# Four-layer MetaFormer: the first token group's work of the second and third expert layers moved into the stage before them

## The reference

```python
t = t + moe(layernorm(t))
scores = t @ gate_w + gate_b;  probs = softmax(scores)       # 4 experts
masked = probs * top2_mask;    masked /= masked.sum() + 1e-9
h = gelu(t @ w1[e] + b1[e]);   y[e] = h @ w2[e] + b2[e]      # 96 -> 384 -> 96
out = sum over e of masked[e] * y[e]
```

## Time and profile before

| | |
|---|---|
| median of 3 runs | 1336.79 us (1335.22 to 1337.23) |
| time of the profiled execution | 1334.63 us |
| its span | 1332.8 us |
| mean granted TensorE clock | 0.929 |
| second expert layer, first DVE instruction to the last addition to X | 523.4 to 703.4 us |
| third expert layer, the same | 904.4 to 1084.7 us |

### The profile page before, as it was taken

How to read it: one execution, slowest core, us unless ns; L and a number is a source line. 1 busy time by engine, 2 the same in 40 slices (tenths; PEclk the granted TensorE clock), 3 DMA queues, 4 the chain that set the end, 5 groups by cost and what they waited for, 6 DMA issues and landing times. The chain is left out here.

```text
span 1332.8 us, 23847 instructions
## 1 busy us (share of the span) xinstructions
PE 1177.9 (88%) x8368; PEld 1020.5 (77%) x8368; DVE 809.8 (61%) x2938; ACT 487.3 (37%) x948; POOL 249.9 (19%) x232
## 2 busy tenths in 40 slices
PE   2979999948999997999996999997999968998776
PEld 2978888937999996888894767676889867886455
DVE  6137676555666653767656665545767667776556
ACT  3524333314554543433331223224333322232542
POOL 3002212121010100221213343322121212111200
PEclk9989999967999998999996999997999988999577
DMA  3201010010000000000000000000000000000000
GB/s 136 76 24 49 14 47 0 0 48 1 1 2 1 2 1 1 1 1 0 0 1 0 1 1 2 1 1 1 1 1 0 0 1 1 1 1 1 3 10 36
DMA packets 11561, 15.67 MB, mean 12 GB/s; under 512 B 7385, under 2 KB 9007, under 8 KB 11346
## 3 DMA queue, kind: packets, MB, share of 16 engines
q1 hardware_dynamic: 10754, 12.86, 3.0%
q10 hardware_dynamic: 720, 1.66, 0.3%
HBM read 11.37 MB, written 3.15 MB: 11 GB/s over the span
## 5 line engine op out<-in xcount | busy, mean ns | idle before, releaser
L663 PEld LDWEIGHTS moe_dn<-all_w,moe_hid 128*128 128x128 f32 x2304 | 270.1, 192 | 5.9
L663 PE MATMUL moe_dn<-all_w,moe_hid 128*128 128x96 f32 x2304 | 271.5, 275 | 0.0
L600 ACT ACTIVATE moe_hid<-moe_up 128x512 f32<-128x512 f32 x288 | 169.7, 598 | 233.9 <-PE moe_up L655 221.8
L653 PE MATMUL moe_up<-moe_xh,moe_w1h 97*128 97x512 f32 x288 | 124.1, 431 | 0.0
L655 PE MATMUL moe_up<-moe_xl,moe_w1h 97*128 97x512 f32 x288 | 115.7, 402 | 0.0
L654 PE MATMUL moe_up<-moe_xh,moe_w1l 97*128 97x512 f32 x288 | 115.5, 401 | 0.0
L558 DVE SCALAR_TENSOR_TENSOR all_X<-moe_dn,moe_gate,all_X 128x96 f32 (+1 forms) x384 | 95.2, 310 | 33.4 <-PE moe_dn L663 29.1
L550 DVE SCALAR_TENSOR_TENSOR all_X<-all_b,moe_gate,all_X 128x96 f32 (+1 forms) x384 | 96.6, 314 | 10.8 <-DVE all_X L558 7.8
L481 POOL TENSOR_TENSOR moe_prob<-moe_euler,moe_logit 128x16 f32<-128x16 f32 x24 | 69.6, 2902 | 141.7 <-DVEq L517 141.7
L1060 PE MATMUL l1c_o<-l1c_vs,l1c_pt 128*128 128x64 f32 x768 | 94.4, 277 | 0.8 <-DVE l1c_ro L853 0.8
L1060 PEld LDWEIGHTS l1c_o<-l1c_vs,l1c_pt 128*128 128x128 f32 x768 | 91.8, 195 | 3.2 <-issue 1.4
(11 more groups left out here) (338 smaller groups left out, 2027.6 us busy)
## 6 DMA issues: line engine op xcount, KB each, us to landing
all_w<-w SPq DMA_DIRECT2D x3, 582.0 KB
all_w<-w SPq DMA_DIRECT2D x3, 576.0 KB
all_X<-x_rows SPq DMA_DIRECT2D x2, 768.0 KB, 6.7
conv_scratch<-all_X SPq DMA_DIRECT2D x2, 768.0 KB, 3.2
all_X<-conv_scratch SPq DMA_DIRECT2D x2, 768.0 KB, 4.7
out_tokens<-l3f_y SPq DMA_DIRECT2D x5, 288.0 KB, 2.1
l0c_band<-band ACTq DMA_DIRECT2D x1, 1248.0 KB, 9.2
all_b<-b SPq DMA_DIRECT2D x3, 192.0 KB
```

The lines of the kernel that those rows point to most:

```text
L600: act.activation(hid[:, n, :], up[n % UPS][:, :], ACT.Gelu).then_inc(hid_done, 1)
L653: pe.matmul(bank, w1h[:, n, :], xh[:, p, :], start=True, stop=False)
L663: last = pe.matmul(dn[e % 2][:, j * C:(j + 1) * C], hid[:, n, j * P:(j + 1) * P], w2[:, n, :], start=(k == 0), stop=(k == KC - 1))
```

## The change

The buffers and small tiles of an expert group are allocated once, ahead of the first expert layer, in a class `ExpertFront`. For layers 1 and 2 the start of the layer is gone: no statistics, normalisation, transposes, weight parts, low tokens or gates of group 0 there, and no memsets or rows of ones, which stay from layer 0. Each of these steps is called inside the program before, at a fixed stage:

- attention: ACT's weight copies at the end of stages 4 to 7, DVE's weight parts at the end of stages 7 to 10, statistics at the end of stage 4, POOL's power in its stage 5, normalisation at the end of stage 6; PE's transposes in stage 14, behind `scores(15, 1)`; ACT's copies, `dve_low` and `dve_gates` at the end of stage 14; PE's gate scores in stage 15, ahead of `values(15, 0)`; POOL's power for the gates behind its loop. The transposes and the scores use the PSUM bank m1, when it is out of use.
- second convolution: ACT's copies of the weights at the end of steps 2 to 5, DVE's parts at the end of steps 3 to 6, statistics at the end of step 3, POOL's power in step 4, normalisation at the end of step 4; transposes in step 7 behind `turn_values(6)`; ACT's copies behind `keys_out(7)`; gate scores behind `sample(6, 1)`; `dve_low` and `dve_gates` at the end of step 7; POOL's power behind its loop. The PSUM bank is tp.

`choose_experts` is the former `gates_of`, with the same operations in the same order. Layer 0 calls the same methods at its own start. The semaphores of group 0 are its own, so the counts of the others go down by one.

```diff
--- before.py
+++ after.py
+def choose_experts(dve, chain, F, scores, p, logit_done, gates_read, exp_done, count):
+    wide = lambda a: a.unsqueeze(2).broadcast_to([P, GT, NE])
+    smax, logit, prob, ge, rank, best = F.smax, F.logit, F.prob, F.ge, F.rank, F.gate[:, p, :, :]
+    chain.sync(dve.tensor_reduce(smax[:, :], scores, AX.X, ALU.max))
+    chain.sync(dve.tensor_tensor(logit[:, :, :], scores, wide(smax[:, :]), ALU.subtract))
+    dve.sem_inc(logit_done, 1)
+    dve.sem_inc(gates_read, 1)
+    for e in range(NE):
+        dve.memset(rank[:, :, e], float(NE - 1 - e))
+    wait(dve, exp_done, count)
...
+class ExpertFront:
...
+    def pool_rstd(self, pool):
+        pool.wait_ge(self.var_done, 1)
+        pool.tensor_tensor(self.rstd[:, :], self.var[:, :], self.mhalf[:, :], ALU.pow).then_inc(self.rstd_done, 1)
+    def pool_exp(self, pool):
+        pool.wait_ge(self.logit_done, 1)
+        pool.tensor_tensor(self.prob[:, :, :], self.euler[:, :].rearrange("p (t e) -> p t e", e=NE),
+                           self.logit[:, :, :], ALU.pow).then_inc(self.exp_done, 1)
+    def dve_stats(self, dve, chain):
+        layernorm_stats(dve, chain, [self.T["X"][:, j, :] for j in range(GT)], self.stats, self.mean, self.var, 1e-5)
+        dve.sem_inc(self.var_done, 1)
+    def dve_apply(self, dve, chain):
+        dve.wait_ge(self.rstd_done, 1)
+        layernorm_apply(dve, chain, [self.T["X"][:, j, :] for j in range(GT)], [self.xn[:, j, :] for j in range(GT)],
+                        self.stats, self.mean, self.rstd).then_inc(self.xn_done, 1)
+    def dve_weights(self, dve, e):
+        dve.wait_ge(self.w_high, e + 1)
+        dve.tensor_tensor(self.expert(self.w1l, e), self.expert(self.w1, e), self.expert(self.w1h, e).bitcast(F32),
+                          ALU.subtract).then_inc(self.w_low, 1)
+    def dve_low(self, dve):
+        dve.wait_ge(self.xt_done, 1)
+        dve.tensor_tensor(self.xl[0:C, 0, :], self.xt[0:C, 0, :], self.xh[0:C, 0, :].bitcast(F32), ALU.subtract
+                          ).then_inc(self.xl_done, 1)
+    def dve_gates(self, dve, chain):
+        dve.wait_ge(self.gates_in, 1)
+        choose_experts(dve, chain, self, self.gp.rearrange("p (t e) -> p t e", e=NE), 0, self.logit_done,
+                       self.gates_read, self.exp_done, 1)
+    def act_weights(self, act, e):
+        if e == 0:
+            act.wait_ge(self.loaded, 64)
+        act.activation(self.expert(self.w1h, e), self.expert(self.w1, e), ACT.Copy).then_inc(self.w_high, 1)
+    def act_tokens(self, act):
+        act.wait_ge(self.turned, 1)
+        act.activation(self.xh[0:C, 0, :], self.tp[0:C, :], ACT.Copy)
+        act.activation(self.xt[0:C, 0, :], self.tp[0:C, :], ACT.Copy).then_inc(self.xt_done, 1)
+    def pe_turn(self, pe):
+        pe.wait_ge(self.xn_done, 1)
+        for j in range(GT):
+            last = pe.transpose(self.tp[0:C, j * P:(j + 1) * P], self.xn[:, j, :], self.T["ident"][:, :])
+        last.then_inc(self.turned, 1)
+    def pe_gates(self, pe):
+        pe.wait_ge(self.loaded, 64)
+        pe.wait_ge(self.xt_done, 1)
+        for j in range(GT):
+            last = pe.matmul(self.gp[:, j * NE:(j + 1) * NE], self.xt[:, 0, j * P:(j + 1) * P], self.gw[:, :],
+                             start=True, stop=True)
+        last.then_inc(self.gates_in, 1)
...
@@ moe
-            with pool.Fori(0, STEPS) as g:
+            with pool.Fori(1, STEPS) as g:
                 rstd_of(g)
                 exp_of(g)
...
-            stats_of(0, chain)
-            apply_of(0, chain)
...
-            gates_of(0, 0, chain)
+            if layer == 0:
+                F.dve_stats(dve, chain)
+                F.dve_apply(dve, chain)
+                for e in range(NE):
+                    F.dve_weights(dve, e)
+                    if e == 0:
+                        F.dve_low(dve)
+                F.dve_gates(dve, chain)
+            dve.wait_ge(T["moe_in"][layer], 64)
             base = chain.n
             steps(dve, step)
...
-            act.wait_ge(T["moe_in"][layer], 64)
-            act.wait_ge(consts, 2)
-            act.activation(xh[C:CB, :, :], xt[C:CB, :, :], ACT.Copy)
-            act.activation(xl[C:CB, :, :], xt[C:CB, :, :], ACT.Copy, scale=0.0)
-            act.activation(expert(w1h, 0), expert(w1, 0), ACT.Copy).then_inc(w_high, 1)
-            turned_out(0, 0)
-            for e in range(1, NE):
-                act.activation(expert(w1h, e), expert(w1, e), ACT.Copy).then_inc(w_high, 1)
+            if layer == 0:
+                act.wait_ge(consts, 2)
+                act.activation(xh[C:CB, :, :], xt[C:CB, :, :], ACT.Copy)
+                act.activation(xl[C:CB, :, :], xt[C:CB, :, :], ACT.Copy, scale=0.0)
+                F.act_weights(act, 0)
+                F.act_tokens(act)
+                for e in range(1, NE):
+                    F.act_weights(act, e)
             gelus(0, 0)
...
             pe.wait_ge(T["moe_in"][layer], 64)
-            turn(0)
-            gates(0, 0)
-            pe.wait_ge(w_low, 1)
+            if layer == 0:
+                F.pe_turn(pe)
+                F.pe_gates(pe)
+                pe.wait_ge(F.w_low, 1)
+                pe.wait_ge(F.xl_done, 1)
             ups(0, 0, 0)
...
@@ -735,6 +815,7 @@
                  "unit_in", "unit_high", "unit_done", "v_in", "v_done", "scored", "maxed", "spread", "nm_in", "nm_high",
                  "nm_done", "st_in", "exped", "valued", "ro_done", "ht_in", "ht_done", "y_in", "added")
         S = {n: s.sem(n) for n in names}
+        F = T["front"].begin(s, T, 1, m1, m1[:, 0:GT * NE])
         block = ctx.enter_context(nc.Block())
         FIRST, SECOND = 8, NT // 2
 
@@ -782,6 +863,11 @@
                 if st == 0:
                     pool.wait_ge(S["x_low"], 4)
                     rstd_of(2, slice(SECOND, NT))
+                if st == 5:
+                    pool.wait_ge(S["x_low"], st + 4)
+                    F.pool_rstd(pool)
+            pool.wait_ge(S["x_low"], NB)
+            F.pool_exp(pool)
 
         @block.vector
         def _(dve):
@@ -908,6 +994,15 @@
                     maxima_low(st + 1)
                 if live(st - 1):
                     add_out(st - 1)
+                if st == 4:
+                    F.dve_stats(dve, chain)
+                if st == 6:
+                    F.dve_apply(dve, chain)
+                if 7 <= st < 7 + NE:
+                    F.dve_weights(dve, st - 7)
+                if st == NB - 2:
+                    F.dve_low(dve)
+                    F.dve_gates(dve, chain)
 
         @block.scalar
         def _(act):
@@ -974,6 +1069,10 @@
                     heads_out(st - 1)
                 if live(st + 1):
                     maxima_high(st + 1)
+                if 4 <= st < 4 + NE:
+                    F.act_weights(act, st - 4)
+                if st == NB - 2:
+                    F.act_tokens(act)
 
         @block.tensor
         def _(pe):
@@ -1106,6 +1205,11 @@
                 if live(st + 2):
                     unit(st + 2, 1)
                     value_tokens(st + 2)
+                if st == NB - 2:
+                    pe.wait_ge(S["unit_done"], 3 * NB)
+                    F.pe_turn(pe)
+                if st == NB - 1:
+                    F.pe_gates(pe)
                 if live(st):
                     values(st, 0)
                 if live(st + 3):
@@ -1194,6 +1298,7 @@
                  "pos_in", "th_done", "dist_done", "hat_done", "bil_done", "val_done", "vt_in", "vt_out", "k_in", "k_out",
                  "kb_done", "q_in", "q_out", "at_in", "at_out", "vb_in", "vb_out", "o_in", "o_out", "y_in", "y_out")
         S = {n: s.sem(n) for n in names}
+        F = T["front"].begin(s, T, 2, tp, tp[:, 0:GT * NE])
         block = ctx.enter_context(nc.Block())
 
         def live(p):
@@ -1251,10 +1356,13 @@
                 offsets_rstd(p)
                 if p in (0, 2):
                     rstd_of(2 + p // 2)
+                if p == 4:
+                    F.pool_rstd(pool)
                 for i in range(2):
                     keys(p, i)
                 for i in range(2):
                     bilinear(p, i)
+            F.pool_exp(pool)
 
         @block.vector
         def _(dve):
@@ -1362,6 +1470,15 @@
                 if p in (0, 2):
                     chain.sync(sums(*BATCHES[2 + p // 2]))
                     token_moments(2 + p // 2)
+                if p == 3:
+                    F.dve_stats(dve, chain)
+                if p == 4:
+                    F.dve_apply(dve, chain)
+                if 3 <= p < NP - 1:
+                    F.dve_weights(dve, p - 3)
+                if p == NP - 1:
+                    F.dve_low(dve)
+                    F.dve_gates(dve, chain)
 
         @block.scalar
         def _(act):
@@ -1450,6 +1569,8 @@
                     outputs_out(p - 1, 1)
                 if live(p + 1):
                     first_tap(p + 1)
+                if 2 <= p < 2 + NE:
+                    F.act_weights(act, p - 2)
 
```

(8 more changed lines are left out.)

167 lines of the change are left out of this document (81 added, 86 removed).

## The result

After the change the kernel takes **1340.58 us** (median of 9 runs, 1338.38 to 1344.36) against 1336.79 (also nine runs, 1335.22 to 1337.23); the ratio is 1.0032, with a 95% interval of 1.0022 to 1.0042. So it is slower by 3.8 us, 0.3%, inside the range and 2.1 us above the forecast. The profiled run took 1340.37 us with a span of 1338.6; against the profiled run of before (1334.63, span 1332.8) that is 5.8 us of span.

A forecast was written before the change was run, and what follows sets the result against it. Bound by TensorE in the stages and chains of small operations at the seams; first seam +1.8 and second -0.1 gave +1.7 us on the median 1336.79, so 1338.5 us, range 1332 to 1345.

The forecast's parts named there:

- Point 1: Gaps before the first up matmuls of layers 1 and 2: 8.55 to 0.6 us, gaining 8.0 us at each seam.
- Point 2: Attention's end: gates on VectorE delay norm_heads(14), so TensorE's values(15, 0) is held, +8.1 us.
- Point 3: Attention stage 14: four transposes on TensorE ahead of values(14, 0), +0.1 us (0 to 0.4).
- Point 4: Second convolution's end: gates wait for GpSimd's power behind bilinear, delaying add_output(6, 0) by 8.4 us, transposes and scores included.
- Point 5: Tails behind both holds: TensorE resumes at half clock, costing 3.0 us in the attention and 2.7 in the convolution.
- Point 6: Expert layers' starts: less time at half clock, gaining 0.9 us at the second layer and 2.6 at the third.
- point 7: First group of each layer: VectorE's bias sums start earlier, so the wait for group 1's tokens goes, gaining 0.7 us each.
- Point 8: Middle stages of attention and convolution: the moved preparation work is mostly covered by idle time, +0.3 us in all (0 to 2).
- the slower one: TensorE returns late from both holds, at half clock when the expert layer begins: 1345, or 1342 with half; chance 0.34.

The follow-up runs named there:

- its own run: Kernel before with only four transposes added in attention stage 14, ahead of values(14, 0): 1336.02 us, ratio 0.9993.
- moving the power: Changed kernel with GpSimd's power for the gates ahead of the last bilinear in the second convolution, not behind the loop: 1336.84 us, ratio 1.0003.
- the run with the attention's seam alone: Change made only between attention and second expert layer; third expert layer starts as in the kernel before: 1344.15 us, ratio 1.0051 against the kernel before.
- the seams run alone: Change made at one seam only, against the kernel before: attention's 1344.15 us, ratio 1.0051; second convolution's 1335.76 us, ratio 1.0002.
- the kernel with the gates behind the heads: Changed kernel with VectorE doing the attention's gates behind norm_heads(14), not ahead of it: 1335.62 us, ratio 0.9983.
- the one with the filler: Changed kernel with 36 unused matmuls of 512 columns between the attention's gate scores and values(15, 0): 1334.07 us, ratio 0.9986.
- the kernel before with the scores alone: Kernel before with only the gate scores' four thin matmuls added in attention stage 15, ahead of values(15, 0): 1344.18 us, ratio 1.0051.
- the split kernel: Changed kernel with gates in two halves at both seams and the power ahead of the last bilinear: 1319.66 us (0.9879); again on another chip 1320.16 (0.9890).

## Why the prediction was right, and where it was not

- **Point 1** (gaps 8.55 to 0.6): 0.33 and 0.32. Right; TensorE's own start behind a switch costs what VectorE's does, 0.3 us less than I took.
- **Point 2** (+8.1): turned_scores(15, 1) is 1.85 us later and values(15, 0) 10.02, so +8.2. Right in place, cause and size.
- **Point 3** (+0.1): nothing that its own run can show. Right.
- **Point 4** (+8.4): add_output(6, 0) from 891.65 to 908.49, less 8.37 of shift before it: 8.5. Right; moving the power gave back 3.15 us of its hold.
- **Point 5** is the step that failed, in the attention's half. I took 3.0 us, half of a stretch of 6 us at half clock, because the stretches of the earlier trace rows last 4.7 to 9.0 us. The tail was at half clock from its first matmul to its last and lost 7.5, and the up matmuls behind it stayed there for some 5 us more. Three of those four stretches held only 12 to 16 long matmuls each; a tail of 64-column values, 96-column mixes and waits is another thing, and no row of mine showed one that had started at half clock. The reason was wrong in part too: I gave it to the idle hold alone, and the scores alone do it as well. The convolution's half was right: 2.7 taken, 2.5 measured. Its 48 short scores matmuls took 5.03 us, 105 ns each, against 62.7 ns at full clock; the clock came back before their end. In the run with the attention's seam alone the same 48 ran at half clock throughout and took 5.38 us, 112 ns each: they did not double but came near.
- **Point 6** (-0.9, -2.6) and **point 7** (-0.7 each): the second layer gave -1.6, as the sum of the two, the third -1.8 of -3.3. By the stretches at half clock (5.3 to 4.9 us, and 6.5 to 3.3) the clock's part was 0.2 and 1.6: the third layer's first up matmuls started at full clock, as forecast, but it fell 1 us later. What is left is 1.4 and 0.2 for point 7, the first above my bound of 1.0, and the 0.4 us over the wait of 0.98 isn't explained; the second is small because TensorE's wait for group 1's tokens had been only 0.41 us at that layer, where I had carried over the 0.98 of the earlier trace rows.
- **Point 8** (0.3): nothing in the attention's middle stages (the shift of 1.8 us is the same from 337 to 495 us), at most 0.7 in the convolution's. Right within its bounds.

Sum by these: first seam +5.8 instead of +1.8, second +0.9 instead of -0.1, near the +5.9 and +0.7 that the profiles of the seams run alone show. The median of the change moved by +3.8 and not by +6.7; in the profiled execution the unchanged layer 3 took back 3.5 us, and whether it does so in the other runs isn't shown. That and the 2.1 us between forecast and median say that the forecast came close partly by luck: one term was short by 4.5 us, and something that I hadn't counted gave most of it back. Of the rivals, the slower one was partly what happened (TensorE "comes back late from both holds"), but it decided in the attention's tail and not at the third layer's start.

By the Trainium skill, "TensorE: Matmul & The Clock Gate", section "Wait — 56ns, not 53.3ns?", the sequencer spends about 62 ns on each matmul when hardware decoding is off, which binds where the array needs less; no run here shows that setting. The 62.7 ns at full clock agree with that figure, and the 112 ns at half clock, less than twice as much, fit it; they did not double, as the prediction had it by that section, but 1.8 times is nearer to doubled than to unchanged. The same page, section "What's actually happening", calls the start at the low clock under 1% of a typical span and not worth fitting. What was measured here is a fall in the middle of a kernel and not a start: 0.92 us of thin matmuls cost 7.1 us, 0.5%, under 1% indeed, but more than the whole effect of this change, so here the measurement decides.

## What to carry to other kernels

When a chain is moved out of a gap, look at what stands behind it in each engine's list: a chain with a round trip to another engine should be cut at the round trip, its first half put where its operand is ready and its second where the engine idles (some 17 us won here at the two seams together, against a loss of 4). Let no thin matmuls and no wait of some microseconds into a dense stretch of short matmuls: price them by the whole stretch behind them at half clock and not by their own time. Where a kernel's runs fall into two groups, compare the difference with that price, and look in the profiles at the stages that were not changed: here they moved by 3.5 and 4.9 us of themselves.

## What the hardware did that I had not expected

- TensorE's granted clock fell from 1.00 to 0.50 with no idle time before it: behind eight passes of 4 columns (1.05 us) in the kernel with the gates behind the heads, in the one with the filler, and in the kernel before with the scores alone. In the split kernel's two profiles it did not. In the run with the attention's seam alone it fell in the unchanged convolution, between 899 and 900 us, with waits of 0.16 and 0.50 us before it.
- Once down, it stayed down through 14.65 us in which TensorE was never idle (519.45 to 534.10: mostly values of 64 columns and mixes of 96, with eight turned scores of 256 and four transposes between them), and came back some 5 us into the up matmuls of 512 columns. With the filler of 512 columns it came back 3.5 us after it had started.
- The first instructions behind a switch of programs start 0.33 us after the last one before it, on TensorE as on VectorE.
